# The grey picture of a vision layer, built by adding transfers in DRAM with planes scaled on ScalarE, and a new order on every engine

## The reference: what is computed

```
gray = einsum('bchw,c->bhw', x, (0.2989, 0.587, 0.114))
edges = conv(gray, scharr)                       # two 3x3 filters, SAME
h = sqrt(square(edges)).sum(axis=1) / 2          # |.| + |.|, halved
n = layernorm(h); xs = n moved by one token
k, v, r = (n*tm + xs*(1-tm)) @ W.T               # three mixes, three weights
wkv = running softmax-like scan of k, v over the tokens (decay w, bonus u)
h = h + (sigmoid(r) * wkv) @ Wo.T
y = layernorm(h); top1 = argmax(y @ Wg.T)        # 8 experts, hidden 64
h = h + expert[top1](y)                          # gelu(y_e @ W1 + b1) @ W2 + b2
```

## Time and profile before

| | us |
|---|---|
| median of three runs | 1226.53 |
| lowest, highest | 1224.15, 1230.5 |
| the profiled execution | 1227.5 |
| its span in the trace | 1225.7 |
| PE busy | 1125.9 (92%) |
| DVE busy | 1063.7 (87%) |
| ACT busy | 813.7 (66%) |
| POOL busy | 10.8 (1%) |
| moved by the transfers | 140.07 MB, mean 114 GB/s |

### The profile page before, as it was taken

The page is one execution under the profiler, slowest core; times in us unless marked ns, Lnnn a source line. Parts: engine busy times, 40 slices in busy tenths (PEclk is TensorE's granted clock), DMA queues, the critical chain, the costliest instruction groups (busy, mean ns, idle before and its releaser), DMA issues.

```text
span 1225.7 us, 16385 instructions
## 1 busy us (share of the span) xinstructions
PE 1125.9 (92%) x5571; PEld 700.5 (57%) x5571; DVE 1063.7 (87%) x1860; ACT 813.7 (66%) x1323; POOL 10.8 (1%) x51
## 2 busy tenths in 40 slices
PE   1477799999999999999999999999999999999997
PEld 0222466665656566656665666566656665566666
DVE  2468899999999999999999999999999999998971
ACT  0245666876767667777677687676767777677652
POOL 3000000000000000000000000000000000000000
PEclk9778899999999999999999999999999999999999
DMA  5855344445553454455434545554344455521001
GB/s 171 195 124 121 90 125 124 101 121 133 141 131 112 118 129 94 127 132 140 128 107 117 131 94 131 132 140 124 105 120 124 100 136 132 140 65 44 18 18 35
DMA packets 145236, 140.07 MB, mean 114 GB/s; under 512 B 9440, under 2 KB 145206, under 8 KB 145206
## 3 DMA queue, kind: packets, MB, share of 16 engines
q1 hardware_dynamic: 145206, 139.69, 44.8%
HBM read 105.96 MB, written 33.69 MB: 114 GB/s over the span
## 4 chain that ended last, share of the span: by engine, by line
PE 74%; ACT 12%; issue 4%; DVE 4%; DMA 4%; SPq 1%; POOL 0%; ACTq 0%; POOLq 0%; DVEq 0%
PE bank L971 22%; PE bank L1110 13%; PE bank L1037 12%; PE bank L965 10%; PE bank L1014 10%; ACT hidden L830 4%; PE bank L1058 3%; ACT normed L845 3%; ACT normed_t L852 2%; ACT normed_hi L859 2%; DMA rows_in<-gray_dram 2%; PE bank L1088 1%; DVE normed_lo L637 1%; DMA gray_dram<-gray 1%; ACT gate L837 1%
## 5 line engine op out<-in xcount | busy, mean ns | idle before, releaser
L1110 PE MATMUL bank<-w_sb,hidden 128*128 128x256 f32 x1024 | 242.0, 383 | 1.0 <-ACT hidden L830 1.0
L1110 PEld LDWEIGHTS bank<-w_sb,hidden 128*128 128x128 f32 x1024 | 184.4, 190 | 35.3 <-issue 7.8
L762 ACT ACTIVATE v_sb<-bank 128x512 f32<-128x512 f32 x64 | 38.3, 598 | 201.6 <-PE bank L971 201.6
L965 PE MATMUL bank<-rows_in,conv_w 102*32 102x512 f32 x1024 | 132.5, 639 | 29.3 <-DMA rows_in<-gray_dram 29.3
L971 PE MATMUL bank<-mixed_r,w_r_t 128*128 128x512 f32 x256 | 122.6, 603 | 7.3 <-DVE mixed_r L536 7.3
L1014 PE MATMUL bank<-w_o_t,rwkv 128*128 128x256 f32 x512 | 124.3, 386 | 2.1 <-DVE rwkv L612 2.1
L1014 PEld LDWEIGHTS bank<-w_o_t,rwkv 128*128 128x128 f32 x512 | 94.6, 190 | 52.3 <-issue 40.0
L971 PE MATMUL bank<-mixed_v,w_v_t 128*128 128x512 f32 x256 | 123.6, 605 | 0.9 <-DVE resid L621 0.9
L971 PE MATMUL bank<-mixed_k,w_k_t 128*128 128x512 f32 x256 | 119.3, 609 | 0.8 <-DVE mixed_k L536 0.8
L1037 PE MATMUL bank<-normed_hi,w_hi 128*128 128x512 f32 x256 | 119.6, 467 | 0.0
L547 DVE TENSOR_TENSOR_SCAN max_state<-neg_exp_w,bank 128x256 f32<-128x256 f32 x128 | 80.6, 671 | 34.6 <-PE bank L971 34.6
(11 more groups left out here) (129 smaller groups left out, 1997.6 us busy)
## 6 DMA issues: line engine op xcount, KB each, us to landing
planes<-in_x_dram SPq DMA_DIRECT2D x64, 768.0 KB, 6.3
rows_in<-gray_dram SPq DMA_DIRECT2D x192, 256.0 KB
gray_dram<-gray SPq DMA_DIRECT2D x64, 258.0 KB, 2.9
out_dram<-resid SPq DMA_DIRECT2D x64, 256.0 KB, 2.2
rows_in<-gray_dram SPq DMA_DIRECT2D x128, 24.0 KB
hidden<-in_L_ffn_W_dram SPq DMA_DIRECT2D x2, 256.0 KB, 9.0
w_sb<-in_L_ffn_W_dram SPq DMA_DIRECT2D x1, 512.0 KB, 4.8
gate<-in_L_attn_Wk_dram SPq DMA_DIRECT2D x1, 256.0 KB, 5.8
```

The source lines that it names most:

```text
L762: act.activation(v_sb[:, 2 * ct:2 * ct + 2, :], pair_view(bank[BANK_V[ct]]), ACT.Copy).then_inc(s_v, 1)
L965: ins = pe.matmul(bank[BANK_EDGE[n]][ROW_TILE * q:ROW_TILE * (q + 1), :], conv_w[0:TAPS, c, :], rows, start=True, stop=True)
L1110: pe.matmul(ps, hidden[:, m, i, rows], w2_sb[:, m, :], start=(m == 0), stop=False)
```

## The change

**The grey picture.** SP loads only red and green into `planes` (four transfers of 256 KB), and copies blue from the input straight into `gray_dram` (two transfers, DRAM to DRAM). ACT multiplies red and green in place by their weights over that of blue (`scaled`, two instructions of 1024 columns). POOL then issues two transfers that add red to `gray_dram`, waits until they have landed, issues two that add green, and SP waits for these before it reads `rows_in`. DVE's two instructions and the tile `gray` are gone. The borders come from one transfer of zeros over all of `gray_dram` at the start.

**The order.** All five queues and nearly all bank numbers differ. The exponentials on ACT now come after both gaps, decay last; the logarithm of `den` moves from the head of a step to the end of the one before; the transpose of the scores and `project_k(0)` stand between the second and third convolution; `mixed_v` is made one stage earlier; ACT reloads its table of functions only where the function changes, not again at each fourth step.

```diff
-        BANK_EDGE, BANK_WO, BANK_K, BANK_V, BANK_R = (3, 5, 1, 2), (0, 1), (7, 1), (4, 1), (3, 2)
+        BANK_EDGE, BANK_WO, BANK_K, BANK_V, BANK_R = (1, 4, 1, 3), (3, 1), (0, 5), (2, 0), (7, 6)
...
             def load_planes(j, c, buf):
 
+                first = j * (UNROLL * 2) + 2 * c
+                for plane in range(2):
+                    for half in range(HALF):
+                        src = x[bass.ds(first, 2), plane, half * P:(half + 1) * P, :]
+                        sp.dma_start(planes[buf][:, 2 * half:2 * half + 2, plane, :], src.rearrange("n p w -> p n w")
+                                     ).then_inc(planes_in[buf], 16)
+
+            def load_blue(j, c, buf):
+
                 for half in range(HALF):
...
+                    src = x[bass.ds(first, 2), 2, half * P:(half + 1) * P, :]
+                    sp.dma_start(gray_rows(buf, half), src.rearrange("n p w -> p n w")).then_inc(blue_in[buf], 16)
...
                 if at.has(LOAD) and not at.first():
-                    wait(sp, s_gray, at.count(LOAD, 1, 1, back=2))
+                    wait(sp, s_green, at.count(LOAD, 16 * HALF, 16 * HALF, back=2))
                     load_planes(at.j, at.u, at.buf(LOAD))
+                if at.has(LOAD) or at.has(GRAY):
+                    wait(sp, s_edge_ps, at.count(LOAD, 4, 4, back=2))
...
+                if at.has(LOAD):
+                    load_blue(at.j, at.u, at.buf(LOAD))
                 if at.has(GRAY):
                     b = at.buf(GRAY)
-                    wait(sp, s_gray, at.count(GRAY, 1, 1))
...
+                    wait(sp, s_green, at.count(GRAY, 16 * HALF, 16 * HALF))
...
+            pool.memset(zeros, 0.0).then_inc(s_zeros, 1)
...
+                wait(pool, blue_in[b], at.dma_count(GRAY, HALF))
+                wait(pool, s_scaled, at.count(GRAY, 2, 2))
+                pool.tensor_tensor(pool_turn[:, :], pool_turn[:, :], pool_turn[:, :], ALU.add).then_inc(s_turn, 1)
+                for half in range(HALF):
+                    pool.dma_start(gray_rows(b, half), planes[b][:, 2 * half:2 * half + 2, 0, :], accum_op=ALU.add
+                                   ).then_inc(s_red, 16)
...
-            def gray_of(at):
...
-                dve.scalar_tensor_tensor(out=gray[:, :, 1:D + 1], in0=planes[b][:, :, 0, :],
...
+            def scaled(c, at):
...
+                act.activation(planes[b][:, :, c, :], planes[b][:, :, c, :], ACT.Copy,
+                               scale=GRAY_WEIGHTS[c] / GRAY_WEIGHTS[2]).then_inc(s_scaled, 1)
```

272 lines of the change are left out of this document (139 added, 133 removed).

## The result

The changed kernel takes 1194.78 us (median of 4 runs, 1192.23 to 1196.99), the kernel before 1225.45 in the same series (1224.15 to 1230.5). The ratio is 0.9742, with a 95% interval of 0.9705 to 0.9778: 2.6% faster. The forecast was 1197 in a range of 1184 to 1232. The total is right, but two terms under it are not: the full steps gave 12.7 us more than forecast and the filling 8.8 us less. That they cancel in large part is luck. The profiled execution took 1192.23 us and its span is 1190.7; before it was 1225.7.

What follows compares the result with a forecast made beforehand. PE was taken as the bound, with DVE close behind. Filling 8.6 plus full steps 23.2 minus draining 0.9 gave 30.9 us off the span of 1225.7, so 1197 us, range 1184 to 1232.

Steps and rivals of the forecast that it cites:

- the full steps: 28 steps from the head of step 6 to step 34: 983.6 us before, 960.4 after, 23.2 us won.
- What bounds the kernel: PE, busy 34.40 of a 35.16 us step, sets the pace; its only stop is 0.93 us ahead of `normed`'s transposes.
- the ceiling is low: Full step: without the stop PE still needs 35.15 - 0.93 = 34.2 us, since no PE work is removed.
- Grey off DVE: Two DVE instructions go, freeing 2.4 us a step; worth nothing by itself in a full step, something in filling.
- A full step of 34.3: PE runs through without a stop; 0.1 us added for 18 changes between kinds of matmul instead of 17.
- The walk: Timing of one full step from its first convolution (T0): nothing late, slacks of 0, 0.7 and 0.8 us on ACT.
- A: Time of one colour's pair of DRAM additions: 6.3 us taken, rows in at T0+25.7, 8.6 us early; may be 10.6.
- Filling, -8.6: Start to the head of step 6: 161.8 us against 170.41, 8.6 us won, give or take 5.
- the additions: Rival: the grey chain to the next step's first convolution binds from A = 10.6 us; 1331 us at A = 13; chance 0.17.
- PE does not run through: Rival: an ACT slack fails or changes of kind cost more; step 34.8 to 35.1 us, 1211 to 1219; chance 0.12.
- The change does not do what it says: Rival: PE's stop moves to another bank, step stays 35.1 us, time about 1220; chance 0.05.
- the rival of POOL and DVE: Each of POOL's four starts a step waits for DVE's running instruction, rows 0.5 us late, 1211 us; chance 0.05.

Runs made afterwards that it cites:

- banks_alone: Kernel before, with only the transposes of `normed` moved to banks 5 and 1 and the waits that follow: 1199.95 us, ratio 0.9799.
- grey_alone: Kernel before with only the new grey (ACT scales, POOL adds in DRAM), old order and banks: 1233.69 us, ratio 1.0071.
- grey_and_banks: Kernel before with the new grey and the new banks for the transposes of `normed`, old order on all engines: 1206.59 us, ratio 0.9837.
- decay_first: Changed kernel with the old grey on DVE behind the second residual, and ACT's decay moved ahead of the reciprocal deviations: 1197.71 us, ratio 0.9765.
- third_addition: Changed kernel with green scaled by half its weight and added twice, a third pair of additions on POOL: 1313.77 us, ratio 1.0715.
- scaled_twice: Changed kernel with two more scalings of 1.0 us on ACT at the head of each step: 1224.43 us, ratio 0.9987.
- grey_later: Changed kernel with the old grey on DVE, placed behind `normalise2`: 1309.6 us, ratio 1.0666.

## Why the prediction was right, and where it was not

The total is right in part by luck: two terms missed in opposite directions. By the prediction's own last sentence, "wrong if the step is above 34.7 or filling wins less than 4 us", the step passes and the filling fails.

- **What bounds the kernel**: right. PE sets the pace, the 0.93 us stop is its only one, and banks_alone with 34.19 confirms the 34.2 of "the ceiling is low".
- **Grey off DVE, "by itself it is worth nothing in a full step"**: right, shown twice (grey_alone, grey_and_banks), and from the other side by decay_first.
- **A full step of 34.3**: the mechanism is right, a size is off. "I add 0.1" for one more change of kind has the wrong sign. The order takes 0.39 us off PE's own work; with the 0.1 this is the 0.48 between 34.3 and 33.82, and so the full steps gave 12.7 us more, 35.9 for 23.2. The working counted the changes and not what stands on either side of them. Also, "the change removes no PE work" was taken as if the work's length did not depend on its order.
- **The walk**: right where it could be read. The decay and `den_scan` meet with nothing idle: ACT's row starts at 593.81 and lasts 1.04 us, DVE's starts at 594.91.

```profile
593.81 1.04 ACT L816 ACTIVATE decay<-decay 128x1024 f32<-128x1024 f32 x1
...
594.91 2.29 DVE L584 TENSOR_TENSOR_SCAN den_state<-decay,fresh 128x1028 f32<-128x1028 f32 x1
```

- **The transfers**: A was put at 6.3; red takes 9.7 and green 6.7 in the median. The reads take 11 to 12 us and not 9.6: the share of 0.11 behind 615 in the earlier trace rows was their tail and not the time after them. So the rows are in at T0+31.2 in the median step instead of T0+25.7. Still early, by 2.6 us instead of 8.6. The estimate of 3.2 us from the Trainium skill (DMA: Bandwidth & Descriptors, Anatomy of one DMA — SWDGE (gpsimd) path) is for the transfer of such bytes, and the page has none for an addition; here an addition of these bytes takes at least twice that, 6.4 us or more.
- **Filling, -8.6**: the step that failed. It was +0.2, below the 4 us that the prediction named as its own limit. Two terms were too small. "`gap(1)` comes 7.3 us after the start of K(0)" was 9.2 and 9.4 us, above all because K ran at or near half clock: in step 4 it stands right behind a wait, in step 3 behind two convolutions that do, where there had been three. And "I put step 3's first convolution 3 us later" was 5.8. That one is only measured: the first grey came late (first convolution at 48.92 for 39.45), and starting its additions earlier did not help.
- **The rivals**: the additions are not the bound, but third_addition shows how near they are: one more costs 119 us. "PE does not run through" did not occur here and is what scaled_twice makes, with 2 us. "The change does not do what it says" did not occur either: PE's stop moved to no other bank. But the half of the change that its title names first, the new grey, gives a full step nothing.

## What to carry to other kernels

A wait that names a semaphore may be a wait for a bank: read which instructions share the buffer before moving work off the engine that is named. Two bank numbers gave 2.0%, and the new grey nothing in a full step. Taking work off the second-busiest engine paid nothing in a full step here, and moving one instruction on ACT paid 0.37 us, since the bound engine waited for what stood behind it; ask for the position, not for the busy share. Where a new order puts a wait directly ahead of the group for which all others wait, price that group at the slow clock as well.

## What the runs showed of the hardware

**A stop on PE can cost twice its length.** Stops of 1.84 and 5.36 us were followed by matmuls at a granted clock of 0.67 and 0.50; the first made a step 3.7 us longer than 33.8. In the full steps of grey_later the stops are 1.7 to 3.2 us, and all but one were followed by a lower clock; the one that was not (2.10 us) was followed by a step 1.3 to 3.3 us shorter than the others. Stops of up to 1.07 us, in before and scaled_twice, left the clock at 1.00.

**DVE can hold up POOL for the rest of an instruction.** In the changed kernel POOL's addition of one element per partition takes 0.18 us in all full steps. In third_addition its third one falls into DVE's scan in many of its steps (timelines of POOL and of DVE):

```profile
878.56 1.80 POOL L415 TENSOR_TENSOR pool_turn<-pool_turn 128x1 f32<-128x1 f32 x1 [4.37 <-DMA gray_dram<-planes]
```

```profile
878.07 2.30 DVE L590 TENSOR_TENSOR_SCAN den_state<-decay,fresh 128x1028 f32<-128x1028 f32 x1
```

POOL's instruction ends at 880.36, DVE's at 880.37. Of that execution's 96 such instructions 15 take over 0.3 us between 40 us and the end, and each of the 15 ends within 0.06 us of the end of a DVE instruction with two inputs in SBUF. The Trainium skill (SBUF — State Buffer, Who interferes with whom) says this of DVE instructions with two SBUF inputs and GpSimd's reads, and the trace agrees. So the rival of POOL and DVE had its mechanism right for these small additions, at 1.8 us or less each; the issuing of the transfers, to which the prediction applied it, takes 2.4 us in either kernel and was not seen to be held up. In the changed kernel's full steps no POOL addition starts in a scan.

**Adding in DRAM.** 512 KB of fp32 added from SBUF by two transfers of POOL take 6.4 to 10.5 us in the changed kernel's full steps, of which POOL is busy with issuing for 2.4. Per byte their packets also take twice the time of the other transfers' on the DMA engines, by the page's part 3 (packets, MB, share of 16 engines; the first line is SP's queue, the second POOL's):

```profile
q1 hardware_dynamic: 129990, 123.84, 42.7%
q0 software_dynamic: 34816, 33.56, 22.3%
```

That is 0.34% per MB for the one and 0.66% for the other.
